# Routing and the first mixture of experts in one block, tiles queued by token group

## The reference, cut to what matters

```python
logits = tokens @ router_w.T                      # 8 experts
probs  = softmax(logits); rw, re = top_k(probs, 2); rw = rw / rw.sum()
out = tokens
for e in range(8):
    h = gelu(tokens @ w1[e] + b1[e])              # 256 -> 256
    y = h @ w2[e] + b2[e]                         # 256 -> 256
    out = out + combine[:, e:e+1] * y
```

## Time and profile before

| | us |
|---|---|
| median of 3 runs | 4547.61 (4541.72 to 4548.05) |
| span of the profiled execution | 4541.9 |
| routing block, in the span | 2105 to 2310 |
| expert block, in the span | 2310 to 2587 |

### The profile page before, as it was taken

One profiled execution on the slowest core, in us unless ns is written; L12 is line 12 of the kernel. 1 busy time (PEld: TensorE's weight loads), 2 busy tenths in 40 slices (PEclk: granted clock), 3 DMA queues, 4 the chain that ended last, 5 costly groups with the idle time before them and its releaser, 6 DMA issues. The chain is left out here.

```text
span 4541.9 us, 47421 instructions
## 1 busy us (share of the span) xinstructions
PE 2760.5 (61%) x12379; PEld 2178.5 (48%) x12379; DVE 2106.8 (46%) x3862; ACT 1140.7 (25%) x2893; POOL 2595.1 (57%) x2731
## 2 busy tenths in 40 slices
PE   5333433433333343344558899958777777768998
PEld 4333333333333333334447644446666666656665
DVE  7322222224222222224635344458888888873444
ACT  6111111110100111112324322234444444424222
POOL 6677777776777777774520142057777777751000
PEclk9655656655555655666679999978888888876999
DMA  4422222222222122223233365344444444430000
GB/s 130 90 53 53 53 53 53 53 53 73 53 53 53 53 53 53 53 53 95 76 119 105 105 216 195 162 146 139 135 140 138 137 140 137 138 119 22 16 16 24
DMA packets 200821, 409.75 MB, mean 90 GB/s; under 512 B 51763, under 2 KB 125123, under 8 KB 193636
## 3 DMA queue, kind: packets, MB, share of 16 engines
q0 software_dynamic: 102016, 246.46, 20.1%
q1 hardware_dynamic: 84868, 153.14, 9.6%
q10 hardware_dynamic: 13664, 6.91, 0.6%
HBM read 305.56 MB, written 104.44 MB: 90 GB/s over the span
## 5 line engine op out<-in xcount | busy, mean ns | idle before, releaser
L722 POOL DMA_INDIRECT ring<-t_gcn,idx x1564 | 1476.5, 944 | 515.6 <-issue 476.0
L783 PE MATMUL psum<-ring,big 128*128 x3328 | 756.0, 420 | 1226.9 <-SPq L730 1216.3
L783 PEld LDWEIGHTS psum<-ring,big 128*128 128x128 f32 x3328 | 704.8, 323 | 1278.1 <-issue 1278.1
L1612 POOL DMA_INDIRECT xs_ring<-t_msg,idx x832 | 797.6, 959 | 380.3 <-issue 249.2
L808 DVE TENSOR_TENSOR big<-big,psum 128x1024 f32 x208 | 254.0, 1221 | 1448.0 <-PE psum L783 1447.2
L749 ACT COPY psum<-zero_sum 128x1024 f32<-128x1024 f32 x208 | 211.0, 1015 | 1761.1 <-DVE big L808 1743.1
L1745 PE MATMUL psum<-xs_ring,a_hot 128*128 128x264 f32 x1456 | 405.9, 439 | 0.0
L1745 PEld LDWEIGHTS psum<-xs_ring,a_hot 128*128 128x128 f32 x1456 | 329.4, 226 | 74.5
L1499 PE MATMUL psum<-big,a_xnt 128*128 128x512 f32 x784 | 355.1, 596 | 0.5 <-ACT a_xnt L1471 0.5
L1404 POOL DMA_INDIRECT a_back<-t_y,m_addr x98 | 97.9, 999 | 438.5 <-POOLq L1208 279.6
L220 DVE TENSOR_TENSOR big<-dloc,psum 128x1024 f32<-128x1024 f32 x208 | 252.4, 1214 | 4.3 <-PEq L702 4.3
(11 more groups left out here) (424 smaller groups left out, 4290.2 us busy)
## 6 DMA issues: line engine op xcount, KB each, us to landing
t_msg<-a_rows SPq DMA_DIRECT2D x49, 1056.0 KB, 3.9
a_near<-t_near SPq DMA_DIRECT2D x52, 512.0 KB, 4.3
ring<-t_gcn,idx POOLq DMA_INDIRECT x1564, 2.5
m_xin<-t_tok SPq DMA_DIRECT2D x105, 128.0 KB, 2.1
t_y<-m_yb SPq DMA_DIRECT2D x105, 128.0 KB, 2.0
xs_ring<-t_msg,idx POOLq DMA_INDIRECT x832
xs_ring<-in_x SPq DMA_DIRECT2D x7, 896.0 KB, 11.9
t_xs<-xs_ring SPq DMA_DIRECT2D x7, 896.0 KB, 6.4
```

The costliest lines, as they stand in the source:

```text
L722: g.indirect_dma_start(out=ring[:, p % HALF_RING * 8 + j, :], out_offset=None, in_=t_gcn[conv], in_offset=bass.IndirectOffsetOnAxis(ap=idx ...
L783: m = t.matmul(opened[:, bass.ds(to[j], ROW_BYTES)].bitcast(F32), hot[q % 2][:, j, :], ring_bytes[:, bass.ds(at[j], ROW_BYTES)].bitcast(F3 ...
L1612: g.indirect_dma_start(out=ring[:, slot, :, :].rearrange("p h c -> p (h c)"), out_offset=None, in_=t_msg, in_offset=bass.IndirectOffsetOnA ...
```

## The change

Both blocks become one. Group 0 and group 1 are routed first; then 105 turns run, and the routing of groups 2 to 6 is spread over them. A slot is queued by the group that fills its tile: slots 0 to 6 need group 0, 7 to 20 group 1, then 14 slots a group, and the last 28 (77 to 104) group 6 and the zero rows. VectorE extends the list after each group (`queue(g)`), and the rows' addresses are mended by `readdress` from the runs of tiles. `t_tok` gets 64 tiles an expert, so that the expert is the tile's number shifted right by 6.

Per slot: up takes `w1` as the stationary operand (four matmuls with 128 columns), so its result is already upright; flip(i), its copy and the bias add on VectorE go, and the bias is an operand of ACT's Gelu (two instructions). Down follows one turn earlier, as down(i-2). `w1` is no longer resident: it is copied once during the first convolution to `t_w1` (two DMAs on ACT's queue, 2 MB), and SP loads 256 KB a slot into 4 buffers.

Per node: PE transposes `acc` directly, the inverse degree goes into VectorE's add, the residual add is an ACT Identity with scale and bias, the root is VectorE's (a shift and three Newton steps), the softmax and its Exp are replaced by one Tanh for all nodes.

The diff, cut to its core (SP, PE, VectorE):

```diff
-                                if i >= XB:
-                                    sp.wait_ge(s_turned.sem, s_turned.base + i - XB + 1)
-                                sp.dma_start(xin[i % XB][:], ...)
-                            if i >= STORE:
-                                sp.wait_ge(s_y.sem, ...); sp.dma_start(y_tiles[n], yb[n % YB][:])
+            XB, YB, WB, PIECE = 6, 4, 4, 512
+            STORE = XB + 4
+            QUEUED = [0] + [2 * GT * g - GT for g in range(1, NG)] + [SLOTS]   # 0 7 21 35 49 63 77 105
+            ROUTED = {GT + 1: 2, **{QUEUED[s] + 13: s + 2 for s in range(1, NG - 2)}}
+                        for i in range(SLOTS + STORE):                         # SP
+                            if i < SLOTS:
+                                if i in QUEUED:
+                                    sp.wait_ge(s_sent[g % 2].sem, ...)         # group g scattered
+                                batch(sp, from_of, 0, i)
+                                if i >= XB:
+                                    sp.wait_ge(s_turned.sem, s_turned.base + i - XB + 1)
+                                sp.dma_start(xin[i % XB][:], tok_tiles[...])
+                                batch(sp, w1_of, 1, i)
+                                if i >= WB:
+                                    sp.wait_ge(s_up.sem, s_up.base + i - WB + 1)
+                                sp.dma_start(w1[i % WB][:], t_w1[...])
+                            ...                                                # 256 KB pieces, steps 54 to 61
+                            if i >= STORE:
+                                n = i - STORE
+                                sp.wait_ge(s_y.sem, s_y.base + n + 1)
+                                sp.dma_start(y_tiles[n], yb[n % YB][:]).then_inc(s_left_y[n % YB].sem, 16)
+                        for i in range(SLOTS + 2):                             # PE
+                            if i < SLOTS:
+                                turn(i)
+                            if 1 <= i <= SLOTS:
+                                up(i - 1)
+                            if i >= 2:
+                                down(i - 2)
+                            if projected_after(i) is not None:
+                                project(projected_after(i))
+                            if upright_after(i) is not None:
+                                upright(upright_after(i))      # waits for add_sums(n - 1)
+                            if norm_at(i) is not None:
+                                flip(norm_at(i))               # waits for normalise(n)
+                            if i and norm_at(i - 1) is not None:
+                                logits(norm_at(i - 1))
+                            if i - 1 in ROUTED:
+                                ranks(ROUTED[i - 1])
+                        for i in range(SLOTS + 2):                             # VectorE
+                            n = norm_at(i)
+                            if n is not None:
+                                if n % GT == 0:
+                                    moments(n // GT)
+                                normalise(n)
+                            if i:
+                                n = projected_after(i - 1)
+                                if n is not None:
+                                    add_sums(n)
+                                    measure(n)
+                            if i in ROUTED:
+                                choose(ROUTED[i])
+                            if i - 2 in ROUTED:
+                                place(ROUTED[i - 2])
+                            if i - 3 in ROUTED:
+                                queue(ROUTED[i - 3])
+                            shares(i)
+                            readdress(i)
+                            if i >= 2:
+                                leave(i - 2)                   # waits for the store of slot i - 6
+                            ...                                # link, scores
```

More of the change, by code:

```diff
@@ L58 @@
 LINK = P + 1
-RS = NT + 1
+RS = 64
 SLOTS = (2 * NPAD + EXPERTS * (P - 1)) // P
-S0 = RS * EXPERTS
+S0 = RS * (EXPERTS - 1) + NT + 1
 EPS = 1e-5
@@ L149, in gnn_ffn_kernel @@
         t_near = nc.dram_tensor("t_near", (PSTEPS // SBS, SBS * P), BF16, kind="Internal").ap()
-        t_tok = nc.dram_tensor("t_tok", ((EXPERTS * (NT + 1) + 1) * P, D), F32, kind="Internal").ap()
+        t_tok = nc.dram_tensor("t_tok", (EXPERTS * RS * P, D), F32, kind="Internal").ap()
         t_y = nc.dram_tensor("t_y", (SLOTS * P, D), F32, kind="Internal").ap()
-        t_b1 = nc.dram_tensor("t_b1", (1, EXPERTS * D), F32, kind="Internal").ap()
+        t_w1 = nc.dram_tensor("t_w1", (EXPERTS, P, KD, D), F32, kind="Internal").ap()
         t_xs = nc.dram_tensor("t_xs", (P, NT * D), F32, kind="Internal").ap()
@@ L752, in _ @@
                                     a.dma_start(t_same8[:, :, q, :], t_same.rearrange("(b j) e -> b j e", j=SBS)).then_inc(s_same.sem, 16)
+                                if q == HEADS:
+                                    for k in range(KD):
+                                        a.dma_start(t_w1[:, :, k, :], m_w1[:, k * P:(k + 1) * P, :]).then_inc(s_same.sem, 16)
                                 if q >= HALVES + 2:
@@ L757, in _ @@
                             store(2 * TURNS - 1)
-                            a.wait_ge(s_same.sem, s_same.base + 16 * HEADS)
+                            a.wait_ge(s_same.sem, s_same.base + 16 * (HEADS + KD))
                             a.wait_ge(s_out.sem, s_out.base + 16 * (2 * TURNS - HALVES))
@@ L819, in gnn_ffn_kernel @@
                 if conv == 0:
-                    s_same.after(16 * HEADS)
+                    s_same.after(16 * (HEADS + KD))
                     s_stage.after(1)
@@ L843, in gnn_ffn_kernel @@
             wt = big[:, 0:KD * TYPES * D].rearrange("p (k c) -> p k c", k=KD)
-            b1r = big[:, NT * ROW - 2 * EXPERTS * D:NT * ROW - EXPERTS * D].rearrange("p (e f) -> p e f", e=EXPERTS)
+            attn = big[:, KD * TYPES * D:KD * TYPES * D + 2 * D].rearrange("p (m f) -> p m f", m=2)
+            spare = KD * TYPES * D + 2 * D
+            weighed = big[:, spare:spare + 512]
+            later = big[:, spare + 512:spare + 512 + 2 * GT * EXPERTS * NG].rearrange("p (c r) -> p c r", c=2 * GT)
@@ new lines, in gnn_ffn_kernel @@
+            XB, YB, WB, PIECE = 6, 4, 4, 512
+            STORE = XB + 4
+            PIECES = KD * TYPES * D // PIECE
+            QUEUED = [0] + [2 * GT * g - GT for g in range(1, NG)] + [SLOTS]
+            SECTION = [sum(QUEUED[s + 1] <= i for s in range(NG)) for i in range(SLOTS)]
+            LOADS = QUEUED[4] + 4
+            ROUTED = {GT + 1: 2, **{QUEUED[s] + 13: s + 2 for s in range(1, NG - 2)}}
+            ALL_CHOSEN = QUEUED[5] + 1
+            LINKS = QUEUED[4]
+            MOVES = QUEUED[6] + 2
```

1005 lines of the change are left out of this document (517 added, 488 removed).

## The result

| | before | after |
|---|---|---|
| median of 4 runs on one chip, us | 4546.15 (4541.72 to 4548.05) | 4709.6 (4704.79 to 4714.93) |
| ratio, 95% interval | | 1.036 (1.0346 to 1.0375) |
| span of the profiled execution, us | 4541.9 | 4713.1 |
| mean granted clock of PE | 0.742 | 0.738 |
| first gather of the next block, us into the span | 2587.6 | 2755.4 |

The change costs 163 us, 3.6%. The next block starts 168 us later, of the 171 us by which the profiled span grew, so nearly the whole loss lies in the merged block. Its turns start about when they were forecast to: turn 0 begins at 2163.95 and turn 7 at 2199.17. What follows is slow turns.

What follows compares the result with a forecast made beforehand. Routing block bound by a chain between engines, expert block by PE. Turn 7 at 2201, sections 3 x 85 + 82, last turns 139 + 4, drain 6: block end 2687, +100 us, 4648 us; range 4545 to 4735.

Steps and rivals of the forecast that it cites:

- Unhindered PE, 1.96 us a turn: PE in the expert turns: transposes 0.22, up 0.87, down 0.87; the flips go, 0.22 us less a turn.
- free turn: A turn with neither normalise nor upright, between routing turns: 2.4 to 4.8 us, taken as 3.3.
- the first rival: Merged block: the store loop doesn't bite and PE sets the pace; 4438 us, chance 0.13.
- The wait that the change adds: SP's queue: the store stands behind the wait for up, and VectorE's y waits for it; L of 3.2 to 4.6 us.
- L: Time from the end of up to y(m), 1.2 us plus the store's landing: 4.4 or, in longer turns, 3.9 us.
- counter-rule of a fixed 2 us: Store landing: about 2 us of a DMA are fixed, so a smaller store wouldn't help; L stays above 3.2.
- Turns with routing work: Turns 7 to 62: normalising turns hold the whole L, 7.0 us; upright alone 6.3; sections 85, 85, 85 and 82 us.
- low-clock sum, 7.6: Turn with normalise when PE runs at 1.2 GHz: 7.6 us, against 6.2 at clock 1.0; 7.0 was taken.
- Plain turns, 3.3 us: Turns 63 to 104: L + 2.06 for two turns, 3.2 us a turn, taken as 3.3; before 2.43.
- Up to turn 7: Start of the merged block: PE starts turn 0 at 2162.5, turn 7 starts at 2201.
- Things taken at nothing: Costed at zero: copy to `t_w1`, choose, place and queue before leave, the last section's scatter wait, ACT's Identity.
- the third rival: Merged block: the loop with the low clock throughout and landings of 3.4 us; 4769 us, chance 0.12.

Runs made afterwards that it cites:

- with the loop open: The changed kernel with SP storing slot i-6 instead of slot i-10 in its step i: 4443.52 us, ratio 0.9774.
- four edits that share only the loop: The changed kernel with stores four steps earlier, 8 y buffers, 5 y buffers or 6 w1 buffers, each alone: 4443.5, 4445.8, 4502.9, 4465.6 us.

## Why the prediction was right

By its own steps:

- **Unhindered PE, 1.96 us a turn.** Right, and only an experiment could show it: with the loop open a free turn is 2430.45 to 2432.43, 1.98 us. The whole of the first rival, "the store loop doesn't bite", was worked out at 4438 us, and the kernel in which it doesn't bite takes 4443.5.
- **The wait that the change adds.** Right, to the instruction: SP waits for up, issues `w1`, then the store; VectorE's add waits for the DMA in 82 of 105 turns. Shown by four edits that share only the loop. L was put at 3.9 us in long turns, with a landing of 2.7. In the turn above, from the end of up's record to the end of the add, are 2369.92 - 2365.84 = 4.1 us, and with the tail of 0.17 that the prediction counts ahead of it 4.3, of which the landing is 3.1. The prediction's counter-rule of a fixed 2 us is written for GpSimd's path, while this store goes by SP's queue; it landed in 1.9 us behind 64 KB and in 2.9 behind 256 KB. No run stored fewer bytes.
- **Turns with routing work: the term that was too small.** The mechanism was right and the size was off. Sections 1 to 4 took 390 us where 337 were forecast. The 24 turns with normalise and without `moments` took 8.2 us on the mean where 7.0 was taken, out of 6.2 at the full clock and 7.6 at the low one: 28 of the 53 us. In all 24 up ran at the low level or fell to it (1.91 us in 22 of them, 1.48 and 1.75 in two). The prediction's own low-clock sum, 7.6, with the landing at 3.1 in place of 2.7 gives 8.0. The 12 free turns of the first three sections took 4.2 where 3.3 was taken, between 2.4 and 4.8; up took 1.76 to 1.92 us in every one: 10 more. The four turns with `moments` took 12.9 on the mean where 10.6 was counted: 9 more, a part of it in the fourth section (15.0), where `link` stands on VectorE too and was put at nothing. The turns that only wait at upright took 6.7 for 6.3, with up at 1.06 us in them. The compromise between two clocks was the choice that failed: the 36 turns, normalising or free, right behind one in which PE had waited for normalise or upright were all slow ones, not half of them. The run with matmuls in the gap gives back 23 us of this.
- **Plain turns, 3.3 us.** They took 161/42 = 3.8. `readdress` was put at half hidden. It isn't, where it stands between a late add and the next one; VectorE in such a turn (start, length, instruction):

```profile
2694.63 0.42 DVE L1385 TENSOR_TENSOR m_yb<-big,psum 128x256 f32<-128x256 f32 x1 [5.06 <-DMA t_y<-m_yb]
2694.97 0.97 DVE L1365 TENSOR_TENSOR big<-m_runstart,m_addrf 128x784 f32<-128x784 f32 x1
2695.97 0.98 DVE L1368 TENSOR_TENSOR big<-big,m_fall 128x784 f32<-128x784 f32 x1
2696.98 0.97 DVE L1370 TENSOR_REDUCE m_downby<-big 128x14 f32<-128x784 f32 x1
2697.86 0.41 DVE L1385 TENSOR_TENSOR m_yb<-big,psum 128x256 f32<-128x256 f32 x1
```

  Two adds that should follow one another stand 3.2 us apart, and the store of the second leaves late. But `readdress` is not the main part: the 14 turns over which it is spread took 3.9 us each, the 14 from 63 to 76, without it but with the last group's `place` and `queue` and the first `scores`, 4.1, and the 11 after it 3.6. What all of them took above the 3.3 I can't divide between this work, the register loads of SP and the clock (0.85 and 0.94 in the two windows).
- **Up to turn 7.** 2201 forecast, 2199.17 measured; turn 0 2162.5 against 2163.95, so the small VectorE steps counted at their spacing came out. That turn 7 fits as well is luck in part: turn 0 took 10.0 us, until 2174 and not 2171, and turns 1 to 6 took 25 us in place of 29.
- **Things taken at nothing.** The copy to `t_w1` and the merged front: the block's first work moved by under 2 us. `choose`, `place` and `queue` stand from the last turn of a section to the fourth of the next; with the loop open these take 2.1 to 3.2 us, so they cost little even without the cover of the wait. SP's waits show no wait for the scatters at the last section. ACT needed one table load of 1.28 us in the whole merged block, for the first Gelu, with 49 Identities and the copies between the Gelus; the one Tanh (2593.7) brought none either, although the prediction notes that it is not listed with Gelu.
- **The sum.** The block was to end at 2687 and ends at 2755, 68 us later: 53 from sections 1 to 4, 18 from the last 42 turns, less 2 at the start. The median moved by 163 us in place of 100, inside the range, and on the side of the third rival (low clock throughout, 4769). Its clock was right for the normalising and the free turns, and wrong for the last 42, where 0.85 and 0.94 were granted; its landing of 3.4 us was not reached. Misses of 53 and 18 us on one side were covered by the width of the range, not by the sum.

What the forecast held least firmly was whether the loop bites at all, and that decides the sign: one turn of slack more for the store, and the 4710 us become 4503, less than before.

## What to carry to other kernels

When a wait is added to a queue that issues in order, list what is queued behind it and follow that to whoever waits for it. Here a load's wait for `up` delayed a store that has nothing to do with it, and 103 us of gain became 163 us of loss. Such a loop opens at any of its links (the order, the buffers of the store, the buffers of the load), and a quick way to see whether it is there is one more buffer: 207 us for 128 KB. Where a loop leaves a gap in PE's work in each turn, add up its turns at the low clock first: here a value between the two clocks was 1.2 us a normalising turn too short.

## What the runs showed of the hardware

- A 128 KB store lands 1.0 us later for 256 KB issued right in front of it on the same queue (2.9 against 1.9 with 64 KB), at a mean of only 95 GB/s over the stretch. With the loop open, at 209 to 241 GB/s, it landed in 3.4 us.
- PE's clock was higher where its gaps were fewer or shorter. In 2199 to 2492 it was granted at 0.70 to 0.74 with the loop, 0.79 with the loop and 64 KB loads, 0.86 with the loop and its gaps partly filled with matmuls that compute nothing, and 0.94 with the loop open. Filling made the kernel 23 us faster.
- The same program takes 15% longer on one chip than on the others (5237 against 4546 us). In the convolutions the add takes 1.22 us on both, and 350 us more of waiting stand ahead of it, mostly put down to "remote"; the rest of the difference was not followed up.
- One `ACT_TABLE_LOAD` of 1.28 us served Gelu, Copy, Identity and one Tanh in the merged block.
